# Graph transformer kernel: one of the edge stage's one-hot matrices is made by ScalarE behind the store, the other compares against PSUM

## The reference

```python
kT = jnp.einsum('nhd,htdo->nhto', k, Watt)
vT = jnp.einsum('nhd,htdo->nhto', v, Wmsg)
kw = kT[src, :, etype]
m = vT[src, :, etype]
a = jnp.einsum('ehd,ehd->eh', kw, q[dst]) * pri[:, etype].T / SQRT_D
att = edge_softmax(a, dst, n)
msg = (m * att[:, :, None]).reshape(-1, H * HS)
hag = jax.ops.segment_sum(msg, dst, num_segments=n)
```

## Time and profile before

| | |
|---|---|
| median of three runs | 5927.63 us |
| lowest and highest | 5916.28 and 5936.7 us |
| span of the profiled execution | 5930.1 us |
| TensorE (matmul) busy | 3888.4 us, 66% |
| VectorE busy | 3581.7 us, 60% |
| ScalarE busy | 1663.9 us, 28% |
| GpSimd busy | 3928.0 us, 66% |
| mean granted TensorE clock | 0.725 of full speed |

### The profile page before, as it was taken

The page is one execution under the profiler, slowest core; times in us unless marked ns, Lnnn a source line. Parts: engine busy times, 40 slices in busy tenths (PEclk is TensorE's granted clock), DMA queues, the critical chain, the costliest instruction groups (busy, mean ns, idle before and its releaser), DMA issues. The chain is left out here.

```text
span 5930.1 us, 75994 instructions
## 1 busy us (share of the span) xinstructions
PE 3888.4 (66%) x19279; PEld 2908.1 (49%) x19280; DVE 3581.7 (60%) x6760; ACT 1663.9 (28%) x4125; POOL 3928.0 (66%) x3959
## 2 busy tenths in 40 slices
PE   2888856666666666665388876666666666666524
PEld 1322346665655655555233335555555555556414
DVE  3554556666666666665666656666666666666657
ACT  0444511111111111111366651222222222222226
POOL 4556467777777777776133337777777777777565
PEclk8888866667666676667688986667766776666656
DMA  7999866666666666666388976666667666666511
GB/s 127 385 355 369 361 197 190 186 183 188 188 187 184 185 184 189 185 183 170 101 360 357 378 294 175 185 186 189 187 185 187 185 191 186 185 185 188 153 40 34
DMA packets 413476, 1234.48 MB, mean 208 GB/s; under 512 B 169651, under 2 KB 222903, under 8 KB 362130
## 3 DMA queue, kind: packets, MB, share of 16 engines
q0 software_dynamic: 202768, 852.28, 44.2%
q1 hardware_dynamic: 121302, 144.14, 12.4%
q10 hardware_dynamic: 89044, 234.66, 10.6%
HBM read 576.49 MB, written 726.60 MB: 220 GB/s over the span
## 5 line engine op out<-in xcount | busy, mean ns | idle before, releaser
L1150 POOL DMA_INDIRECT kv_e_<-table_d,row_s_ x1568 | 1541.1, 983 | 485.1 <-issue 480.3
L1150 POOL DMA_INDIRECT kv_e<-table_d,row_s x1568 | 1536.7, 980 | 491.8 <-issue 486.0
L1331 PE MATMUL sum_ps<-pv,to_rank 128*128 128x136 f32 x3136 | 622.8, 384 | 149.7 <-DVE pv L1244 149.7
L1331 PE MATMUL sum_ps_<-pv_,to_rank_ 128*128 128x136 f32 x3136 | 614.7, 381 | 149.5 <-DVE pv_ L1244 149.5
L1331 PEld LDWEIGHTS sum_ps<-pv,to_rank 128*128 128x128 f32 x3136 | 603.6, 288 | 178.0 <-issue 178.0
L1331 PEld LDWEIGHTS sum_ps_<-pv_,to_rank_ 128*128 128x128 f32 x3136 | 595.5, 285 | 177.8 <-issue 177.8
L1297 PE MATMUL qe_ps<-q_w,of_rank 128*128 (+1 forms) x3168 | 536.6, 327 | 155.9 <-DVE kq L1223 122.7
L1297 PE MATMUL qe_ps_<-q_w_,of_rank_ 128*128 (+1 forms) x3168 | 530.6, 326 | 126.0 <-DVE kq_ L1223 100.4
L1223 DVE TENSOR_TENSOR kq<-kv_e,qe_ps 128x512 f32<-128x512 f32 x392 | 267.6, 683 | 523.0 <-DMA kv_e<-table_d,row_s 522.9
L1223 DVE TENSOR_TENSOR kq_<-kv_e_,qe_ps_ 128x512 f32<-128x512 f32 x392 | 267.8, 683 | 521.1 <-DMA kv_e_<-table_d,row_s_ 521.0
L1297 PEld LDWEIGHTS qe_ps<-q_w,of_rank 128*128 128x128 f32 x3168 | 469.9, 230 | 211.0 <-issue 180.2
(11 more groups left out here) (402 smaller groups left out, 6488.5 us busy)
## 6 DMA issues: line engine op xcount, KB each, us to landing
part_d<-sums ACTq DMA_DIRECT2D x105, 1088.0 KB, 4.8
part_d<-sums_ ACTq DMA_DIRECT2D x98, 1088.0 KB, 4.8
local_b<-local_d SPq DMA_DIRECT2D x100, 512.0 KB, 6.2
local_b_<-local_d SPq DMA_DIRECT2D x100, 512.0 KB, 5.6
kv_e<-table_d,row_s POOLq DMA_INDIRECT x1568, 2.8
kv_e_<-table_d,row_s_ POOLq DMA_INDIRECT x1568, 2.8
q_w<-q_d SPq DMA_DIRECT2D x100, 64.0 KB
q_w_<-q_d SPq DMA_DIRECT2D x100, 64.0 KB
```

The source lines that it names most:

```text
L1150: pool.indirect_dma_start(out=kv_e[:, b, t, :], out_offset=None, in_=table_d, in_offset=bass.IndirectOffsetOnAxis(ap=row_s[:, b, t:t + 1], ...
L1331: last = pe.matmul(sum_ps[:, n % 3, (t - t0) * REC:(t - t0 + 1) * REC], to_rank[:, b, t, :], pv[:, b, t, :], start=True, stop=True)
```

## The change

The instructions that make `of_rank` go from VectorE to ScalarE and from one comparison to two passes over the same data: the absolute value of partition number minus rank, and then the positive part of one minus that, in place. The eight instructions of chunk c+2 stand behind the store of chunk c, where VectorE had the four between L1238 and L1244. The first two chunks' stand ahead of ScalarE's loop, behind the fill in layer 0. `to_rank` is compared with a copy of `lane` that is put in a bank of PSUM at the stage's start; since PSUM has eight banks, the sums have two in place of three.

```diff
--- before.py
+++ after.py
@@ -1108,24 +1108,29 @@
         ends_max = sb(st, "ends_max", [P, 2, 2])
         pv = sb(st, "pv", [P, 2, CT, REC])
         sums = sb(st, "sums", [P, 2, CT, REC])
-        UB = 3
+        UB, SB = 3, 2
         batches = [(a, min(a + UB, CT)) for a in range(0, CT, UB)]
+        PER = len(batches) // SB
+        assert len(batches) % SB == 0
         qe_ps = ps(st, "qe_ps", [P, CT * D])
         turn_ps = ps(st, "turn_ps", [P, 4, P])
-        sum_ps = ps(st, "sum_ps", [P, 3, 512])
+        sum_ps = ps(st, "sum_ps", [P, SB, 512])
+        fixed_ps = ps(st, "fixed_ps", [P, 512])
+        lane_ps = fixed_ps[:, 0:P]
         with nc.Block() as block:
             two = lambda n: [sem(f"e_{n}{b}") for b in range(2)]
             (s_idx, s_q, s_loc, s_flag, s_of, s_to, s_qe, s_kq, s_score, s_turn, s_turned, s_scan, s_below, s_exp,
              s_prob, s_pcol, s_used, s_ends, s_endsd, s_out, s_go) = (two(n) for n in (
                  "idx", "q", "loc", "flag", "of", "to", "qe", "kq", "score", "turn", "turned", "scan", "below",
                  "exp", "prob", "pcol", "used", "ends", "endsd", "out", "go"))
-            s_win = sem("e_win")
+            s_win, s_fixed = sem("e_win"), sem("e_fixed")
+            s_apart = two("apart")
             if not l:
                 s_blank, s_filled = sem("e_blank"), sem("e_filled")
             s_kv = [[sem(f"e_kv{b}{q}") for q in range(4)] for b in range(2)]
             s_pv = [[sem(f"e_pv{b}{q}") for q in range(4)] for b in range(2)]
-            s_sum = [sem(f"e_sum{k}") for k in range(3)]
-            s_sumc = [sem(f"e_sumc{k}") for k in range(3)]
+            s_sum = [sem(f"e_sum{k}") for k in range(SB)]
+            s_sumc = [sem(f"e_sumc{k}") for k in range(SB)]
             fwd_d = start_d[0:EP].rearrange("(c t e) -> c t e", t=CT, e=P)
             rev_d = start_d[1:EP + 1].rearrange("(c t e) -> c t e", t=CT, e=P)
             loc_d = local_d.rearrange("(c a n) -> c a n", a=1, n=CT * P)
@@ -1193,15 +1198,22 @@
                 for b in range(2):
                     sp.wait_ge(s_q[b], (NCH // 2 + 1) * 16)
 
-            def spread_ranks(dve, c, b, i):
-                dve.wait_ge(s_loc[b], (i + 1) * 16)
+            def spread_ranks(act, c, b, i, first=False):
+                act.wait_ge(s_loc[b], (i + 1) * 16)
+                if not first:
+                    act.wait_ge(s_qe[b], i * 4)
                 for q in range(4):
-                    dve.tensor_scalar(of_rank[:, b, q * QT:(q + 1) * QT, :].rearrange("p t e -> p (t e)"),
-                                      local_b[:, b, q * QT * P:(q + 1) * QT * P], part[:], None, ALU.is_equal).then_inc(s_of[b], 1)
+                    rows = of_rank[:, b, q * QT:(q + 1) * QT, :].rearrange("p t e -> p (t e)")
+                    act.activation(rows, local_b[:, b, q * QT * P:(q + 1) * QT * P], ACT.Abs, scale=-1.0, bias=part[:, 0:1]
+                                   ).then_inc(s_apart[b], 1)
+                for q in range(4):
+                    rows = of_rank[:, b, q * QT:(q + 1) * QT, :].rearrange("p t e -> p (t e)")
+                    act.wait_ge(s_apart[b], i * 4 + q + 1)
+                    act.activation(rows, rows, ACT.Relu, scale=-1.0, bias=ones[:, 0:1]).then_inc(s_of[b], 1)
 
             def place_edges(dve, c, b, i, q):
                 dve.wait_ge(s_used[b], ONE + i)
-                dve.tensor_tensor(to_rank[:, b, q * QT:(q + 1) * QT], lane[:].unsqueeze(1).broadcast_to([P, QT, P]),
+                dve.tensor_tensor(to_rank[:, b, q * QT:(q + 1) * QT], lane_ps.unsqueeze(1).broadcast_to([P, QT, P]),
                                   local_c[:, ds(c * CT + q * QT, QT)].unsqueeze(2).broadcast_to([P, QT, P]), ALU.is_equal
                                   ).then_inc(s_to[b], 1)
 
@@ -1209,8 +1221,8 @@
             def _(dve):
                 if not l:
                     dve.memset(sums[:, 1], 0.0).then_inc(s_blank, 1)
-                for b in range(2):
-                    spread_ranks(dve, b, b, 0)
+                dve.tensor_copy(lane_ps, lane[:]).then_inc(s_fixed, 1)
+                dve.wait_ge(s_fixed, 1)
                 for q in range(4):
                     place_edges(dve, 0, 0, 0, q)
                 with dve.Fori(0, NCH // 2) as i:
@@ -1236,7 +1248,6 @@
                                                ).then_inc(s_scan[b], 1)
                         dve.wait_ge(s_scan[b], i * 2 + 2)
                         dve.tensor_tensor(below[:], score_t[:], rank_max[:], ALU.subtract).then_inc(s_below[b], 1)
-                        spread_ranks(dve, c + 2, b, i + 1)
                         dve.wait_ge(s_pcol[b], i + 1)
                         for q in range(4):
                             ts = slice(q * QT, (q + 1) * QT)
@@ -1255,6 +1266,8 @@
                     for c in range((NG - 1) * GT // CT, NCH):
                         act.dma_start(out_d[c:c + 1, :, :, :].rearrange("a j t f -> j (a t) f"), sums[:, 1]).then_inc(s_filled, 16)
                     act.wait_ge(s_filled, 16 * (NCH - (NG - 1) * GT // CT))
+                for b in range(2):
+                    spread_ranks(act, b, b, 0, first=True)
                 with act.Fori(0, NCH // 2) as i:
                     for b in range(2):
                         c = i * 2 + b
@@ -1276,15 +1289,16 @@
                         for n, (t0, t1) in enumerate(batches):
                             if n == len(batches) - 1:
                                 act.wait_ge(s_used[b], ONE + i + 1)
-                            elif n % 3 == 2:
-                                act.wait_ge(s_sum[2], c + 1)
+                            elif n % SB == SB - 1:
+                                act.wait_ge(s_sum[SB - 1], c * (PER - 1) + n // SB + 1)
                             else:
-                                act.wait_ge(s_sum[n % 3], c * 2 + n // 3 + 1)
-                            last = act.copy(sums[:, b, t0:t1, :], sum_ps[:, n % 3, 0:(t1 - t0) * REC].rearrange("p (t f) -> p t f", f=REC)
-                                            ).then_inc(s_sumc[n % 3], 1)
-                        for k in range(3):
-                            act.wait_ge(s_sumc[k], ONE + c * 2 + 2)
+                                act.wait_ge(s_sum[n % SB], c * PER + n // SB + 1)
+                            last = act.copy(sums[:, b, t0:t1, :], sum_ps[:, n % SB, 0:(t1 - t0) * REC].rearrange("p (t f) -> p t f", f=REC)
+                                            ).then_inc(s_sumc[n % SB], 1)
+                        for k in range(SB):
+                            act.wait_ge(s_sumc[k], ONE + c * PER + PER)
                         act.dma_start(out_d[ds(c, 1), :, :, :].rearrange("a j t f -> j (a t) f"), sums[:, b]).then_inc(s_out[b], 16)
+                        spread_ranks(act, c + 2, b, i + 1)
                 for b in range(2):
                     act.wait_ge(s_out[b], ONE + NCH // 2 * 16)
                     act.wait_ge(s_endsd[b], ONE + NCH // 2 * 16)
@@ -1326,11 +1340,11 @@
                         pe.wait_ge(s_pcol[b], i + 1)
                         for n, (t0, t1) in enumerate(batches):
                             pe.wait_ge(s_pv[b][(t1 - 1) // QT], ONE + i + 1)
-                            pe.wait_ge(s_sumc[n % 3], ONE + c * 2 + n // 3)
+                            pe.wait_ge(s_sumc[n % SB], ONE + c * PER + n // SB)
                             for t in range(t0, t1):
-                                last = pe.matmul(sum_ps[:, n % 3, (t - t0) * REC:(t - t0 + 1) * REC], to_rank[:, b, t, :],
+                                last = pe.matmul(sum_ps[:, n % SB, (t - t0) * REC:(t - t0 + 1) * REC], to_rank[:, b, t, :],
                                                  pv[:, b, t, :], start=True, stop=True)
-                            last.then_inc(s_sum[n % 3] if n < len(batches) - 1 else s_used[b], 1)
+                            last.then_inc(s_sum[n % SB] if n < len(batches) - 1 else s_used[b], 1)
         st.close()
```

## The result

The changed kernel takes 6250.8 us (median of 4 runs, 6248.4 to 6260.2) against 5926.7 us (5916.3 to 5936.7) of the kernel before: ratio 1.0539, 95% interval 1.0524 to 1.0554. It is slower, as forecast, but by 324 us and not by 600: the loop closed as described, and a turn of it takes 22.2 us, not 23.6. The time lies within the forecast's ends of 6220 to 6760 us, close to the lower one.

A forecast was written before the change was run, and what follows sets the result against it. GpSimd's gathers bound the kernel at 20.55 us a chunk; a loop of 23.6 us would replace them, adding 296 us in layer 0, 288 in layer 1 and 15 at the start: +599, 6527 us, range 6220 to 6760.

The forecast's parts named there:

- the loop: Transpose to store, eight ACTIVATEs, 24 matrix instructions, next transpose: a closed circle, 23.6 us a chunk against 20.55 before.
- The two sources of slow gathers: GpSimd's gathers beside VectorE's comparisons of L1199 and L1204: about half the 0.55 us a chunk of excess each.
- rival A: Not slower: TensorE's clock is up, GpSimd stays the bound, gathers gain 0.55 us a chunk; 5836 us; chance 0.07.
- rival B: ScalarE's table loads: if Abs and Exp share no set, two loads a chunk, 6775 to 7025 us; chance 0.03.
- 24 make 5.4 us, all at 1.2 GHz: TensorE's 24 matrix instructions before the transpose, after over 6 us idle, at 0.225 us each.
- the chunk of 1819 us: Chunk of the kernel before, transpose at 1819.34, store issued at 1832.31: 12.97 us, the measure for the circle's length.
- The sign that I had given for a wrong price of the loop: Eight ACTIVATEs taking other than 4.4 to 5.7 us, or the 24 matrix instructions other than 5.4.
- my 0.15 for the banks: Between transpose and store: 0.15 us a chunk added for two PSUM banks for the sums.
- The lower end: Shortest circle: ACTIVATE spacing 0.53 (-0.65) and sums of 5.82 us (-0.95), 22.0 us a chunk, 6217 us.
- Rival C: Slower for less: the circle exists but some link overlaps, 20.7 to 22.0 us, 5960 to 6215 us; chance 0.06.
- The start: Layer 0's prologue: two one-hot sets on ScalarE follow the part_d fill, first transpose moves to about 816, +15 us.
- its side question: Whether VectorE's two-SBUF-input comparison of L1204 slows gathers; if only L1199 counted, 5890 us instead of 5836.

The follow-up runs named there:

- the woven one: Changed kernel with ScalarE's same eight passes moved ahead, four before the first copy of sums, four behind one copy each: 5836.8 us, 0.9836 of the kernel before.
- the two woven kernels: Changed kernel with ScalarE's eight passes moved ahead among its copies, lane in PSUM (5836.8 us) or read from SBUF again (5887.6 us).

## Why the prediction was right, and where its size was off

**What bounded the kernel: right.** The two sources of slow gathers were those named, about equal, and the removal of one is worth 59 us (the kernel with VectorE's comparison back, against its own 5932.6 us of before) and that of both 96 us (the woven one). Expected ahead of these two runs were 53 and, with the start's 10 us taken off, 98; the prediction itself had 92 for both (rival A).

**The loop: right in every link, wrong in the size of one.** The forecast's terms against the means of the changed kernel's 69 turns:

| term | forecast, us | measured, us |
|---|---|---|
| transpose to store | 12.62 | 11.83 (11.10 and 12.58 in turn) |
| store to first ACTIVATE | 0.44 | 0.49 |
| eight ACTIVATEs and handover | 5.16 | 5.10 |
| 24 matrix instructions | 5.4 | 4.77 (4.25 and 5.27 in turn) |
| sum | 23.6 | 22.18 |

The ACTIVATEs took 709 and 706 ns, bf16 or fp32 input alike, and followed each other after 0.61 us. The Trainium skill (ScalarE: Activation LUTs, "What ACT_TABLE_LOAD costs") gives 280 ns + 0.833 ns a column for one pointer operand, 707 ns; the trace agrees. The table loads are those of before, 49 at the copy of the row numbers (L1276 now), where TensorE's 24 instructions cover them, so rival B fell.

**The step that failed** is "24 make 5.4 us, all at 1.2 GHz", with its companion, that the sums would run as in the chunk of 1819 us. The sign that I had given for a wrong price of the loop ("the 24 other than 5.4") came true: they took 4.77 us in the mean. Of the 280.5 us that the span's growth fell short of the forecast (318.5 against 599), 275 are in the 194 intervals, 1.42 us each; the rest is the 9.8 us between the layers, less 1.3 at the start and 3.1 behind. The 1.42 us divide into three: 0.63 in the 24 instructions, 0.63 in first sum to store (7.00 us against 7.48 in that chunk, which with my 0.15 for the banks made 7.63), and 0.16 in transpose to first sum (4.83 against 5.49 less 0.5).

The 24 instructions and the sums go with TensorE's clock. In every second turn first sum to store takes 7.63 us, just as forecast, and in the others 6.38. The chunk of 1819 us was itself a long one for its kernel, whose mean is 7.11: for this term I took one chunk where the mean stood open. That the 0.16 us are the clock too, and how much of my 0.15 for the banks is real, was not separated. The slices of the changed kernel show the clock (columns as above):

```profile
1810.00:1811.00 1.00, 1.00 (x7) 1.00 (x7) 0.00 (x0) 0.00 (x0) 0.69 (x2) 0.50 0.43 131
1811.00:1812.00 1.00, 1.00 (x8) 1.00 (x8) 0.00 (x0) 0.00 (x0) 0.85 (x1) 0.70 0.43 131
1812.00:1813.00 1.00, 1.00 (x11) 0.83 (x9) 0.00 (x0) 0.00 (x0) 0.84 (x1) 1.00 0.37 107
...
1817.00:1818.00 1.00, 0.55 (x4) 0.55 (x5) 1.00 (x3) 0.00 (x0) 0.01 (x1) 1.00 0.93 332
1818.00:1819.00 1.00, 1.00 (x9) 1.00 (x8) 1.00 (x3) 0.50 (x1) 0.93 (x1) 0.71 0.52 120
...
1834.00:1835.00 1.00, 1.00 (x6) 0.71 (x4) 0.00 (x0) 0.00 (x0) 0.76 (x1) 0.50 0.32 86
1835.00:1836.00 1.00, 1.00 (x6) 0.84 (x6) 0.00 (x0) 0.01 (x1) 0.69 (x2) 0.75 0.29 82
```

The burst that starts at 1808.48 is at 1.2 GHz as forecast, but the clock rises within 1811 to 1812, after some 3 us of work, and stays up through the transpose into the first sums. The burst of 1829.41 rises only within 1835 to 1836, after 6 us. I had taken one burst, which rose late, for the rule; the same work meets either, in turn.

That the time still fell within the forecast's ends was partly luck. The lower end, 22.0 us a turn, was made of shorter spacing between the ACTIVATEs and of the shortest sums; the ACTIVATEs kept the middle value, and the 24 instructions, which these ends did not vary, made up for them. Rival C, 20.7 to 22.0 us for a link that overlaps, missed the measured 22.18 by little, but its mechanism is not there: no link overlaps another.

**The start: right.** Forecast +15, measured +16.3 us: ScalarE began the ones at 801.58, behind the fill. Between the layers 9.8 us came back, which I had not counted. Before, GpSimd's last gathers and the wait for them ran right up to the end (8.97 us of waiting ahead of the last transpose); now they are done long before. That this explains the 9.8 us is argued, not tried.

**Rival A** fell as a forecast, but its mechanism is real: with TensorE kept busy the kernel is back at the time of before. On its side question, an instruction with two SBUF inputs does slow these gathers: 51 us between the two woven kernels. The Trainium skill (SBUF — State Buffer, "SBUF: two separate sides") says so only against GpSimd instructions that read SBUF, and for descriptor writing it names only the two-port modes. Whether a gather's issue counts as reading SBUF is not shown here; the measurement decides for a slowdown.

## What to carry to other kernels

Idle time of an engine is not room for work at that place in its order: follow what the work's consumer holds up, and if the circle comes back to the work's own start, its length is a lower bound of the period, whatever the engines' shares say. Move such work to where its engine waits for something that does not depend on it; here the same eight instructions cost 377 us behind the store, against the kernel with the comparison on VectorE and all else alike (6250.8 and 5873.4 us), and gained 37 us between the copies (5836.8 us). And a loop through TensorE should be priced at both levels of its clock, as a range.

## What the runs showed of the hardware that I had not expected

More work in a loop can make it faster: ten ACTIVATEs behind the store took 6166 us and eight 6251 us, and 20 useless products a chunk saved 330 us, in both cases with a higher granted clock (0.78 and 0.83 against 0.69 from 1000 to 2400 us). Four ACTIVATEs and six took the same time, 5917 us, the four with all turns of 20.46 to 20.50 us, the six with turns of 19.2 and 21.7 us in alternation.
